# A graph transformer on one core: one low half of FF1 moved from VectorE to GpSimd, an eps step moved, GpSimd's passes cut by graph

## The chip, the core and the metric

The kernel runs on one core of a Trainium2 chip. The metric is device time in microseconds (us). Engines are named as the profile names them: PE is TensorE (matmuls; PEld its weight loads), DVE is VectorE, ACT is ScalarE, POOL is GpSimd, SP is SyncE, which issues the DMAs.

## The reference, cut to what matters

128 independent graphs of 128 nodes with 256 features each. One attention layer ("layer 0") with a residual comes first, then three transformer layers, each of which computes, for every graph:

```python
attn = softmax(where(mask, leaky(x @ aw[:d] [:, None] + x @ aw[d:] [None, :] + b), -inf))
h = layernorm(x + attn @ x, g1[l], beta1[l])                       # eps 1e-5
ff = gelu(h @ W1[l] + b1[l]) @ W2[l] + b2[l]                       # 256 -> 1024 -> 256
x = layernorm(h + ff, g2[l], beta2[l])
```

The output is the result of the third layer plus a residual. All of it is float32; the kernel splits matmul operands into a high and a low half (below).

## The kernel before, in words

**Units and steps.** Four graphs (`T = 4`) form a group, and there are 32 groups. A unit is one group in one of the three layers, so there are 96 units, and one step of the program works on unit `s` in its feed-forward part, while it prepares unit `s + 1` (aggregation, first layernorm), unit `s + 2` (scores and softmax), unit `s + 3` (dot products with the attention vector), and finishes unit `s - 1` (second layernorm). Eight groups are taken through layer 0 of the three, then the same eight through the next, and so on: 24 steps for eight groups (`PER`). Beside this the attention layer 0 of a later group passes through four stages, `early`, `middle`, `late`, `end` (`v0` to `v3`); from step 2 to step 71 a group enters every third step. So steps come in three kinds, which this text calls **A** (`s` = 2, 5, 8, ...: `early` of a new group and `end` of the one before), **B** (`s` = 3, 6, 9, ...: `middle`) and **C** (`s` = 4, 7, 10, ...: `late`). Steps after 73 carry none of it and are called plain.

**Split matmuls.** W1, W2, the normalized input and the gelu are each kept as a float32r high half and a low half (value minus high half), and a product is hi\*hi + hi\*lo + lo\*hi. FF1 (L553, 48 matmuls of 512 columns) makes eight chunks of 128 hidden features x 512 nodes in four PSUM banks; `turn` says which bank a chunk uses, so chunks 4 to 7 reuse the banks of chunks 1, 0, 2 and 3. For each chunk ACT computes the gelu twice from the bank: L674 rounds it into `g_hi`, L676 writes it in full back to the bank. DVE then makes `g_lo` = bank - `g_hi` (L843, `g_low(c)`). PE may overwrite a bank only when its `g_low` is done (L549), and FF2 (L568, 4 x 24 matmuls of 256 columns) waits in its first quarter, chunk by chunk, for `g_lo` of that chunk (L565).

**Order.** Each engine's order is written out by hand in its `body(st)`, and everything between engines is a semaphore. On DVE a step is: sums of the FF2 result (L888), `g_low(0)`, the aggregate's scaling (L904), statistics (L817), `g_low(1)`, mean, variance and eps of the first layernorm (L822, L828), the biases of the softmax (L779 to L791), `g_low(2)`, normalization of `ub` (L927, "z"), `g_low(3)`, in an A step the statistics of the new group's input, `g_low(4)`, `g_low(5)`, in an A step their mean and eps, the statistics of the second layernorm, `g_low(6)`, their mean and eps, `g_low(7)`, and then the rest, which ends with the dot products (L812).

**On POOL** a step is: the power -1/2 for the first layernorm (`rs1`, L1023), which DVE's z waits for; gain and shift of `h` (L1036, L1038) after z; the powers of the other layernorms; masks; and last `affine`, gain and shift of the output `xo` of unit `s - 1` (L356, L358), and in the last layer `residual` (L366). `affine` waits until DVE's dot products of this step are done, so it usually runs into the start of the next step. Each of these passes is one instruction over 128x1024 elements.

Of the kernel before, what the change touches and what calls it, by code (L numbers as in the profile page):

```python
# [13 lines left out]
P = 128  # L14
T = 4
# [21 lines left out]
def build(nc, x, adj, w_fc, w_attn0, attn_w, attn_b, w1, b1, w2, b2, g1, beta1, g2, beta2, out):  # L37
# [44 lines left out]
    with ctx:  # L82
# [37 lines left out]
        et = sb("et", [P, T, P])  # L120
        wfc = et[0:O, :, :].rearrange("p t m -> p (t m)")[:, 0:D]
# [114 lines left out]
        g_lo_ready = sem("g_lo_ready")  # L236
        ff2_done = sem("ff2_done")
# [39 lines left out]
        def live(u):  # L277

            return 0 <= u < U
# [41 lines left out]

        def low_done(eng, st, s, c):

            eng.wait_ge(g_lo_ready, st.nth(s, C, c + 1))
# [22 lines left out]
        def all_graphs(row):  # L347
            return row.unsqueeze(1).to_broadcast((P, T, D))

        def affine(eng, st, u):  # L350


            l = layer(u)
            last = l == L - 1
            eng.wait_ge(z2_ready, st.nth(u))
            eng.tensor_tensor(xo[:, :, :], xo[:, :, :], all_graphs(g2_row[:, l, :]), ALU.mult).then_inc(xo_scaled, 1)  # L356
            eng.wait_ge(xo_scaled, st.nth(u))
            eng.tensor_tensor(xo[:, :, :], xo[:, :, :], all_graphs(beta2_row[:, l, :]),  # L358
                              ALU.add).then_inc(xo_shifted if last else xo_ready, 1)

        def residual(eng, st, u):

            if layer(u) == L - 1:
                eng.wait_ge(xo_shifted, st.nth0(group(u)))
                eng.wait_ge(r_in, 16 * st.nth0(group(u)))
                eng.tensor_tensor(xo[:, :, :], xo[:, :, :], xin[1][:, :, :], ALU.add).then_inc(xo_ready, 1)  # L366
# [121 lines left out]
        def _(pe):  # L488
# [42 lines left out]
            def body(st):  # L531
# [4 lines left out]
                def hidden(c):  # L536
# [11 lines left out]
                    if c >= 4:  # L548
                        low_done(pe, st, s, turn[:4].index(turn[c]))  # L549
# [76 lines left out]
        def _(act):  # L626
# [29 lines left out]
            def body(st):  # L656
# [11 lines left out]
                if live(s):  # L668

                    for c in range(C):  # L670
                        act.wait_ge(ff1_done, st.nth(s, C, c + 1))
                        block_in = bank[turn[c]][:, :]
                        bias = b1_eff[:, layer(s), c:c + 1]
                        act.activation(g_hi[:, c, :], block_in, ACT.Gelu, bias=bias).then_inc(g_hi_ready, 1)  # L674
                        act.wait_ge(g_hi_ready, st.nth(s, C, c + 1))
                        act.activation(block_in, block_in, ACT.Gelu, bias=bias).then_inc(gelu_done, 1)  # L676
                        if c == 1:
                            turned0()
                else:
                    turned0()  # L680
# [4 lines left out]
                if live(s + 2):  # L685
                    act.wait_ge(cc_ready, st.nth(s + 2))
                    exps(e1, ps_s, cc).then_inc(e12_ready, 1)
# [45 lines left out]
        def _(dve):  # L733
# [102 lines left out]
            def body(st):  # L836
# [3 lines left out]
                def g_low(c):  # L840
                    if live(s):
# [69 lines left out]
                g_low(1)  # L911
                if live(s + 1):
                    if not live(s):
                        dve.tensor_copy(spare[:, 2:2 + T], neg_half[:, :])
# [21 lines left out]
                g_low(5)  # L936
                if v0 is not None:
# [4 lines left out]
                second_statistics()  # L942
                g_low(6)
                second_variance()
                g_low(7)
# [58 lines left out]
        def _(pool):  # L1004
# [20 lines left out]
            def body(st):  # L1025
                s = st.s
                v0, v1, v2, v3 = early(s), middle(s), late(s), end(s)
                if live(s + 1):
                    inverse_root(st.nth, s + 1, ve1, rs1, ve1_ready, rs1_ready)
                if live(s + 1):  # L1030
# [5 lines left out]
                    pool.tensor_tensor(h[:, :, :], ub[:, :, :], all_graphs(g1_row[:, l, :]), ALU.mult).then_inc(h_scaled, 1)  # L1036
                    pool.wait_ge(h_scaled, st.nth(s + 1))
                    pool.tensor_tensor(h[:, :, :], h[:, :, :], all_graphs(bb_row[:, l, :]), ALU.add).then_inc(h_ready, 1)  # L1038
# [53 lines left out]
```

## Time and profile before

| | |
|---|---|
| median of 3 runs | 2913.54 us (2911.18 to 2914.14) |
| the profiled execution | 2913.99 us, span 2912.2 us |
| PE busy | 2706.7 us (93%) |
| DVE busy | 2348.0 us (81%) |
| ACT busy | 2148.6 us (74%) |
| POOL busy | 1393.0 us (48%), 806 instructions |
| granted PE clock, mean over the span | 0.969 |

How to read it: the span runs from the first to the last instruction; what the execution's own time has beyond it (1.8 us) lies around it. The first 250 us fill the pipeline. From about 330 us on steps repeat almost to the nanosecond, in periods of three, so one period can be read in detail and multiplied.

### The profile page before, as it was taken

How to read it: one execution, taken by the hardware profiler on the slowest of the kernel's cores; microseconds unless marked ns; L12 is line 12 of the kernel's file. 1: busy time of each engine (PE TensorE's matmuls, PEld its weight loads, DVE VectorE, ACT ScalarE, POOL GpSimd, SP SyncE). 2: the span in 40 equal slices, each digit the busy share in tenths (PEclk: the TensorE clock that was granted, in tenths of full speed). 3: DMA queues.
4: the chain of work that ended last, by engine and by line, in shares of the span. 5: the costliest groups of instructions: out<-in, count | busy, mean ns of one | idle time of the engine just before them, and what ended most of it. 6: DMA issues, size and time to landing. Idle time of an engine off the chain costs nothing.

```text
span 2912.2 us, 52128 instructions
## 1 busy us (share of the span) xinstructions
PE 2706.7 (93%) x16868; PEld 2430.6 (83%) x16868; DVE 2348.0 (81%) x8540; ACT 2148.6 (74%) x3978; POOL 1393.0 (48%) x806
## 2 busy tenths in 40 slices
PE   4268999999999999999999999999999999999998
PEld 3157888888888888888888889888888998999987
DVE  5577798888889888888888888888888887777774
ACT  3357787878778777877777877878787777777775
POOL 2233454444555454444555444545455544444454
PEclk9678999999999999999999999999999999999999
DMA  5322212121322122121223122121222111111211
GB/s 170 111 89 75 78 62 75 63 75 62 97 71 77 62 75 66 63 77 51 90 75 98 61 70 62 58 77 61 89 75 91 57 57 50 50 36 47 64 62 51
DMA packets 120307, 209.64 MB, mean 72 GB/s; under 512 B 12992, under 2 KB 85728, under 8 KB 120032
## 3 DMA queue, kind: packets, MB, share of 16 engines
q1 hardware_dynamic: 120032, 206.26, 22.1%
q8 instruction: 137, 2.24, 0.3%
q14 instruction: 138, 1.13, 0.1%
HBM read 118.15 MB, written 88.08 MB: 71 GB/s over the span
## 4 chain that ended last, share of the span: by engine, by line
PE 74%; DVE 16%; ACT 4%; issue 3%; DMA 1%; POOL 1%; SPq 0%; DVEq 0%; POOLq 0%; ACTq 0%
PE bank L568 35%; PE bank L553 28%; PE ps_u L528 5%; DVE st L817 4%; DVE g_lo L843 4%; PE ps_u L605 2%; PE ps_s L523 2%; DVE ub L904 1%; PE ps_s L515 1%; DVE ve L828 1%; DVE ub L927 1%; DMA xin<-in_x 1%; DVE mv L822 1%; ACT g_hi L674 1%; ACT bank L676 1%
## 5 line engine op out<-in xcount | busy, mean ns | idle before, releaser
L568 PE MATMUL bank<-w_hi,g_hi 128*128 128x256 f32 x3072 | 904.5, 294 | 49.9 <-DVE g_lo L843 49.7
L568 PE MATMUL bank<-w_hi,g_lo 128*128 128x256 f32 x3072 | 875.0, 285 | 0.0
L568 PE MATMUL bank<-w_lo,g_hi 128*128 128x256 f32 x3072 | 874.2, 285 | 0.0
L674 ACT ACTIVATE g_hi<-bank,b_eff 128x512 fp32r<-128x512 f32 x768 | 529.6, 690 | 461.8 <-PE bank L553 456.9
L843 DVE TENSOR_TENSOR g_lo<-bank,g_hi 128x512 fp32r<-128x512 f32 x768 | 518.9, 688 | 211.6 <-ACT bank L676 198.9
L553 PE MATMUL bank<-zt_hi,w_hi 128*128 128x512 f32 x1536 | 646.8, 421 | 12.0 <-DVE vb L888 9.8
L568 PEld LDWEIGHTS bank<-w_hi,g_hi 128*128 128x128 f32 x3072 | 590.0, 192 | 61.8 <-DVE g_lo L843 60.9
L1023 POOL TENSOR_TENSOR rs<-ve,neg_half 128x4 f32<-128x4 f32 x256 | 262.4, 1027 | 726.2 <-DVE ve L828 718.4
L553 PE MATMUL bank<-zt_hi,w_lo 128*128 128x512 f32 x1536 | 608.6, 396 | 0.0
L553 PE MATMUL bank<-zt_lo,w_hi 128*128 128x512 f32 x1536 | 607.7, 396 | 0.0
L568 PEld LDWEIGHTS bank<-w_lo,g_hi 128*128 128x128 f32 x3072 | 590.9, 192 | 0.7
L568 PEld LDWEIGHTS bank<-w_hi,g_lo 128*128 128x128 f32 x3072 | 589.7, 192 | 0.0
L676 ACT ACTIVATE bank<-bank,b_eff 128x512 f32<-128x512 f32 x768 | 508.4, 662 | 25.0
L356 POOL TENSOR_TENSOR xo<-xo,g_row 128x1024 f32<-128x1024 f32 x95 | 226.9, 2388 | 532.4 <-DVE elu_r L985 245.8
L553 PEld LDWEIGHTS bank<-zt_hi,w_hi 128*128 128x128 f32 x1536 | 290.9, 189 | 72.8 <-DVE vb L888 11.7
L553 PEld LDWEIGHTS bank<-zt_hi,w_lo 128*128 128x128 f32 x1536 | 290.3, 189 | 68.2
L553 PEld LDWEIGHTS bank<-zt_lo,w_hi 128*128 128x128 f32 x1536 | 291.4, 190 | 59.2
L1036 POOL TENSOR_TENSOR hb<-ub,g_row 128x1024 f32<-128x1024 f32 x96 | 231.7, 2413 | 222.5 <-DVE ub L927 222.5
L812 DVE CUSTOM_DVE_ANT_0 ub<-xb,aw_row 128x256 f32<-128x256 f32 x768 | 289.4, 432 | 1.3 <-issue 1.0
L646 ACT ACTIVATE e<-ps_s,cc 128x128 f32<-128x128 f32 x512 | 195.5, 382 | 82.3 <-DVE cc L791 81.2
L888 DVE TENSOR_TENSOR vb<-bank,hb 128x512 f32<-128x512 f32 x192 | 129.9, 689 | 142.6 <-PE bank L568 139.0
L1038 POOL TENSOR_TENSOR hb<-hb,bb_row 128x1024 f32<-128x1024 f32 x96 | 229.4, 2389 | 7.5
(95 smaller groups left out, 4265.8 us busy)
## 6 DMA issues: line engine op xcount, KB each, us to landing
xb<-x_scratch SPq DMA_DIRECT2D x96, 512.0 KB, 4.4
x_scratch<-xo SPq DMA_DIRECT2D x69, 512.0 KB, 5.0
xin<-in_x SPq DMA_DIRECT2D x40, 512.0 KB, 4.4
r_scratch<-elu_r SPq DMA_DIRECT2D x32, 512.0 KB, 3.0
xin<-r_scratch SPq DMA_DIRECT2D x32, 512.0 KB, 6.0
out<-xo SPq DMA_DIRECT2D x32, 512.0 KB, 5.3
m<-m_scratch SPq DMA_DIRECT2D x96, 128.0 KB, 2.0
x_scratch<-h SPq DMA_DIRECT2D x24, 512.0 KB, 2.7
```

Of the source, the lines that this page charges most:

```text
L356: eng.tensor_tensor(xo[:, :, :], xo[:, :, :], all_graphs(g2_row[:, l, :]), ALU.mult).then_inc(xo_scaled, 1)
L528: pe.matmul(ps_u[t // 2][:, t % 2 * D:(t % 2 + 1) * D], weights[:, t, :], rows[:, t, :], start=True, stop=True).then_inc(done, 1)
L553: mm = pe.matmul(bank[turn[c]][:, :], w[:, l, k, c * P:(c + 1) * P], z[:, k, :], start=(n == 0), stop=(n == 3 * K1 - 1))
L568: mm = pe.matmul(y, g[:, c, r * P:(r + 1) * P], w[:, l, c, :], start=(c == 0 and n == 0), stop=(c == C - 1 and n == 2))
L646: act.activation(e[:, t, :], src, ACT.Exp, bias=cols[:, 0, t:t + 1])
L674: act.activation(g_hi[:, c, :], block_in, ACT.Gelu, bias=bias).then_inc(g_hi_ready, 1)
L676: act.activation(block_in, block_in, ACT.Gelu, bias=bias).then_inc(gelu_done, 1)
L812: dve.tensor_tensor_reduce(junk[:, j, :], rows[:, t, :], vec(j), 1.0, 0.0, ALU.mult, ALU.add, dot[:, j, t:t + 1]).then_inc(ready, 1)
L843: dve.tensor_tensor(g_lo[:, c, :], bank[turn[c]][:, :], g_hi[:, c, :].bitcast(F32), ALU.subtract).then_inc(g_lo_ready, 1)
L1023: pool.tensor_tensor(rs[:, :], ve[:, :], neg_half[:, :], ALU.pow).then_inc(rs_ready, 1)
L1036: pool.tensor_tensor(h[:, :, :], ub[:, :, :], all_graphs(g1_row[:, l, :]), ALU.mult).then_inc(h_scaled, 1)
L1038: pool.tensor_tensor(h[:, :, :], h[:, :, :], all_graphs(bb_row[:, l, :]), ALU.add).then_inc(h_ready, 1)
```

## The change

It does five things. (1) ACT's second gelu of chunk 1 goes to `g_full`, which is the buffer `e1` (idle at that time) seen as 128x512, not back to the PSUM bank; ACT waits for the last reader of `g_full` before it writes there. (2) `g_low(1)` leaves DVE and becomes POOL's first instruction of a step, 128x512, with a semaphore of its own (`g_lo_pool`). (3) PE's FF1 chunk 4, which reuses chunk 1's bank, waits for ACT's second gelu of chunk 1 and no longer for `g_low(1)`. (4) On DVE, mean and eps of the new group's input (A steps) move from ahead of the second layernorm's statistics to behind `g_low(7)`; the small copy to `spare` that stood there in the fill alone is now issued ahead of the first layernorm's mean in every step. (5) Every 128x1024 pass of POOL (`affine`, `residual`, gain and shift of `h`), and the three of DVE at the very end, are issued as four passes of 128x256.

```diff
+        g_full = e1.rearrange("p t m -> p (t m)")
...
+        POOL_LOW = (1,)
...
         def low_done(eng, st, s, c):
-            eng.wait_ge(g_lo_ready, st.nth(s, C, c + 1))
+            here = sum(k in POOL_LOW for k in range(c + 1))
+            if c + 1 - here:
+                eng.wait_ge(g_lo_ready, st.nth(s, C - len(POOL_LOW), c + 1 - here))
+            if here:
+                eng.wait_ge(g_lo_pool, st.nth(s, len(POOL_LOW), here))
...
-        def all_graphs(row):
-            return row.unsqueeze(1).to_broadcast((P, T, D))
+        def by_graph(eng, dst, src, other, op):
+            for t in range(T):
+                ins = eng.tensor_tensor(dst[:, t, :], src[:, t, :], other(t), op)
+            return ins
...
-            eng.tensor_tensor(xo[:, :, :], xo[:, :, :], all_graphs(g2_row[:, l, :]), ALU.mult).then_inc(xo_scaled, 1)
+            by_graph(eng, xo, xo, lambda t: g2_row[:, l, :], ALU.mult).then_inc(xo_scaled, 1)
             eng.wait_ge(xo_scaled, st.nth(u))
-            eng.tensor_tensor(xo[:, :, :], xo[:, :, :], all_graphs(beta2_row[:, l, :]),
-                              ALU.add).then_inc(xo_shifted if last else xo_ready, 1)
+            by_graph(eng, xo, xo, lambda t: beta2_row[:, l, :], ALU.add).then_inc(xo_shifted if last else xo_ready, 1)
...
                     if c >= 4:
-                        low_done(pe, st, s, turn[:4].index(turn[c]))
+                        owner = turn[:4].index(turn[c])
+                        if owner in POOL_LOW:
+                            pe.wait_ge(gelu_done, st.nth(s, C, owner + 1))
+                        else:
+                            low_done(pe, st, s, owner)
...
-                        act.activation(block_in, block_in, ACT.Gelu, bias=bias).then_inc(gelu_done, 1)
+                        if c in POOL_LOW:
+                            if c > POOL_LOW[0]:
+                                act.wait_ge(g_lo_pool, st.nth(s, len(POOL_LOW), POOL_LOW.index(c)))
+                            elif live(s - 1):
+                                act.wait_ge(g_lo_pool, st.nth(s - 1, len(POOL_LOW)))
+                            act.activation(g_full, block_in, ACT.Gelu, bias=bias).then_inc(gelu_done, 1)
+                        else:
+                            act.activation(block_in, block_in, ACT.Gelu, bias=bias).then_inc(gelu_done, 1)
...
                 if live(s + 2):
                     act.wait_ge(cc_ready, st.nth(s + 2))
+                    if live(s):
+                        act.wait_ge(g_lo_pool, st.nth(s, len(POOL_LOW)))
                     exps(e1, ps_s, cc).then_inc(e12_ready, 1)
...
-                g_low(1)
                 if live(s + 1):
-                    if not live(s):
-                        dve.tensor_copy(spare[:, 2:2 + T], neg_half[:, :])
+                    dve.tensor_copy(spare[:, 2:2 + T], neg_half[:, :])
                     moments(st1, mv1, mv1_ready)
...
                 g_low(5)
+                second_statistics()
+                g_low(6)
+                second_variance()
+                g_low(7)
                 if v0 is not None:
                     if not live(s):
                         dve.tensor_copy(spare[:, 2:2 + T], neg_half[:, :])
                     moments(st4, mv4, mv4_ready)
                     variance(st.nth0, v0, mv4, ve4, mv4_ready, ve4_ready)
-                second_statistics()
-                g_low(6)
-                second_variance()
-                g_low(7)
...
+                def g_low(c):
+                    if live(s):
+                        pool.wait_ge(gelu_done, st.nth(s, C, c + 1))
+                        pool.tensor_tensor(g_lo[:, c, :], g_full, g_hi[:, c, :].bitcast(F32),
+                                           ALU.subtract).then_inc(g_lo_pool, 1)
+
+                g_low(POOL_LOW[0])
                 if live(s + 1):
                     inverse_root(st.nth, s + 1, ve1, rs1, ve1_ready, rs1_ready)
...
-                    pool.tensor_tensor(h[:, :, :], ub[:, :, :], all_graphs(g1_row[:, l, :]), ALU.mult).then_inc(h_scaled, 1)
+                    by_graph(pool, h, ub, lambda t: g1_row[:, l, :], ALU.mult).then_inc(h_scaled, 1)
```

The order of instructions, DVE in an A step, from the first layernorm's statistics on. Before:

```order
936 L817 BN_STATS st<-ub 128x6 x4
937 L843 TENSOR_TENSOR g_lo<-bank,g_hi 128x512
938 L822 BN_AGGR mv<-st 128x2 x4
939 L828 TENSOR_SCALAR ve<-mv 128x4
940 L779 TENSOR_REDUCE small<-ps_s 128x4
```

and with the change:

```order
935 L840 BN_STATS st<-ub 128x6 x4
936 L935 COPY spare<-neg_half 128x4
937 L845 BN_AGGR mv<-st 128x2 x4
938 L851 TENSOR_SCALAR ve<-mv 128x4
939 L802 TENSOR_REDUCE small<-ps_s 128x4
```

The `g_lo` subtraction has gone and a copy of 128x4 to `spare` stands in its place. Further on in the same step, from the statistics of the new group's input (`xin`) to `g_low(7)`. Before:

```order
949 L817 BN_STATS st<-xin 128x6 x4
950 L843 TENSOR_TENSOR g_lo<-bank,g_hi 128x512 x2
951 L822 BN_AGGR mv<-st 128x2 x4
952 L828 TENSOR_SCALAR ve<-mv 128x4
953 L817 BN_STATS st<-vb 128x6 x4
954 L843 TENSOR_TENSOR g_lo<-bank,g_hi 128x512
955 L822 BN_AGGR mv<-st 128x2 x4
956 L828 TENSOR_SCALAR ve<-mv 128x4
957 L843 TENSOR_TENSOR g_lo<-bank,g_hi 128x512
```

and with the change:

```order
948 L840 BN_STATS st<-xin 128x6 x4
949 L866 TENSOR_TENSOR g_lo<-bank,g_hi 128x512 x2
950 L840 BN_STATS st<-vb 128x6 x4
951 L866 TENSOR_TENSOR g_lo<-bank,g_hi 128x512
952 L845 BN_AGGR mv<-st 128x2 x4
953 L851 TENSOR_SCALAR ve<-mv 128x4
954 L866 TENSOR_TENSOR g_lo<-bank,g_hi 128x512
955 L845 BN_AGGR mv<-st 128x2 x4
956 L851 TENSOR_SCALAR ve<-mv 128x4
```

The first of the two pairs of mean (`mv`) and eps (`ve`) has moved from ahead of the statistics of `vb` to behind the last subtraction; the next instruction after it is `zt_lo` in both.

POOL, from the end of an A step (`affine`) into the B step after it, with the semaphores that each waits for. Before:

```order
103 L356 TENSOR_TENSOR xo<-xo,g_row 128x1024 [waits z2_ready,dots0_ready,dots_ready]
104 L358 TENSOR_TENSOR xo<-xo,beta_row 128x1024 [waits xo_scaled]
105 L1023 TENSOR_TENSOR rs<-ve,neg_half 128x4 [waits ve1_ready]
106 L1036 TENSOR_TENSOR hb<-ub,g_row 128x1024 [waits v_done,z_ready]
107 L1038 TENSOR_TENSOR hb<-hb,bb_row 128x1024 [waits h_scaled]
```

and with the change:

```order
131 L358 TENSOR_TENSOR xo<-xo,g_row 128x256 [waits z2_ready,dots0_ready,dots_ready]
132 L358 TENSOR_TENSOR xo<-xo,g_row 128x256 x3
133 L358 TENSOR_TENSOR xo<-xo,beta_row 128x256 [waits xo_scaled]
134 L358 TENSOR_TENSOR xo<-xo,beta_row 128x256 x3
135 L1053 TENSOR_TENSOR g_lo<-e,g_hi 128x512 [waits gelu_done]
136 L1044 TENSOR_TENSOR rs<-ve,neg_half 128x4 [waits ve1_ready]
137 L358 TENSOR_TENSOR hb<-ub,g_row 128x256 [waits v_done,z_ready]
138 L358 TENSOR_TENSOR hb<-ub,g_row 128x256 x3
139 L358 TENSOR_TENSOR hb<-hb,bb_row 128x256 [waits h_scaled]
140 L358 TENSOR_TENSOR hb<-hb,bb_row 128x256 x3
```

Between `affine` and the power for the first layernorm (`rs`, waiting for `ve1_ready`) there is now the subtraction of chunk 1, and each pass is four instructions, of which the first carries the wait.

## Rows read from the trace of the kernel before

**Rows 1.** Busy time of PE, from the page.

```profile
PE 2706.7 (93%) x16868; PEld 2430.6 (83%) x16868; DVE 2348.0 (81%) x8540; ACT 2148.6 (74%) x3978; POOL 1393.0 (48%) x806
```

**Rows 2.** Waits of PE from 300 us on: us in total, times, longest.

```profile
PE bank L568 <- DVE g_lo L843: 48.7, 45, 1.9
```

**Rows 3.** Timeline of ACT: start, us, engine, line, operation [idle before <-releaser].

```profile
1042.45 0.69 ACT L674 ACTIVATE g_hi<-bank,b_eff 128x512 fp32r<-128x512 f32 x1 [2.26 <-PE bank L553]
...
1046.30 0.66 ACT L676 ACTIVATE bank<-bank,b_eff 128x512 f32<-128x512 f32 x1
...
1072.61 0.69 ACT L674 ACTIVATE g_hi<-bank,b_eff 128x512 fp32r<-128x512 f32 x1 [1.85 <-PE bank L553]
...
2641.67 0.69 ACT L674 ACTIVATE g_hi<-bank,b_eff 128x512 fp32r<-128x512 f32 x1 [2.33 <-PE bank L553]
...
2667.97 0.69 ACT L674 ACTIVATE g_hi<-bank,b_eff 128x512 fp32r<-128x512 f32 x1 [2.35 <-PE bank L553]
```

**Rows 4.** Timeline of PE in a step A, around its wait.

```profile
1057.17 0.28 PE L568 MATMUL bank<-w_lo,g_hi 128*128 128x256 f32 x1
1057.29 0.28 PE L568 MATMUL bank<-w_hi,g_lo 128*128 128x256 f32 x1
1059.31 0.39 PE L568 MATMUL bank<-w_hi,g_hi 128*128 128x256 f32 x1 [1.74 <-DVE g_lo L843]
```

**Rows 5.** Windows on PE: us, busy us (x instructions), granted clock, DMA share, GB/s.

```profile
1056.20:1059.60 3.40, 1.66 (x14) 1.00 0.00 0
1059.65:1063.05 3.40, 3.07 (x15) 0.50 0.00 0
1230.30:1233.70 3.40, 2.94 (x23) 1.00 0.00 0
```

**Rows 6.** Timeline of DVE in the same step A, and a copy in the B after it.

```profile
1047.60 0.69 DVE L843 TENSOR_TENSOR g_lo<-bank,g_hi 128x512 fp32r<-128x512 f32 x1
...
1048.61 0.17 DVE L828 TENSOR_SCALAR ve<-mv 128x4 f32<-128x4 f32 x1
...
1050.69 1.37 DVE L927 TENSOR_SCALAR ub<-ub,mv,rs 128x256 f32<-128x256 f32 x4
...
1055.22 0.37 DVE L822 BATCH_NORM_AGGREGATE mv<-st 128x2 f32<-128x6 f32 x4
1055.62 1.50 DVE L828 TENSOR_SCALAR ve<-mv 128x4 f32<-128x4 f32 x1
1057.04 1.39 DVE L817 BATCH_NORM_STATS2 st<-vb 128x6 f32<-128x256 f32 x4
...
1059.65 0.69 DVE L843 TENSOR_TENSOR g_lo<-bank,g_hi 128x512 fp32r<-128x512 f32 x1
...
1090.32 0.51 DVE L781 COPY small<-dots 128x4 f32<-128x4 f32 x1
```

**Rows 7.** Timeline of POOL through steps A and B.

```profile
1039.45 2.40 POOL L356 TENSOR_TENSOR xo<-xo,g_row 128x1024 f32<-128x1024 f32 x1 [9.64 <-DVE elu_r L985]
...
1054.71 2.39 POOL L1038 TENSOR_TENSOR hb<-hb,bb_row 128x1024 f32<-128x1024 f32 x1
...
1065.66 1.01 POOL L1023 TENSOR_TENSOR rs<-ve,neg_half 128x4 f32<-128x4 f32 x1 [3.83 <-DVE ve L828]
1066.63 0.19 POOL L1018 TENSOR_TENSOR spare<-neg_half 128x1 f32<-128x1 f32 x1
...
1071.68 2.37 POOL L356 TENSOR_TENSOR xo<-xo,g_row 128x1024 f32<-128x1024 f32 x1 [2.62 <-DVE dots L812]
...
1088.88 1.93 POOL L1048 TENSOR_SCALAR m_new<-m_new 128x512 bf16<-128x512 bf16 x1
```

**Rows 8.** Timelines of POOL and DVE in a step B of the last layer.

```profile
905.79 2.39 POOL L366 TENSOR_TENSOR xo<-xo,xin 128x1024 f32<-128x1024 f32 x1
...
906.85 1.36 DVE L828 TENSOR_SCALAR ve<-mv 128x4 f32<-128x4 f32 x1
```

**Rows 9.** Timeline of PE: first matmul of chunk 7 in a step B.

```profile
1083.81 0.40 PE L553 MATMUL bank<-zt_hi,w_hi 128*128 128x512 f32 x1
```

More of the change, by code:

```diff
@@ L236, in build @@
         g_lo_ready = sem("g_lo_ready")
+        g_lo_pool = sem("g_lo_pool")
         ff2_done = sem("ff2_done")
@@ L365, in residual @@
                 eng.wait_ge(r_in, 16 * st.nth0(group(u)))
-                eng.tensor_tensor(xo[:, :, :], xo[:, :, :], xin[1][:, :, :], ALU.add).then_inc(xo_ready, 1)
+                by_graph(eng, xo, xo, lambda t: xin[1][:, t, :], ALU.add).then_inc(xo_ready, 1)
         block = ctx.enter_context(nc.Block())
@@ L840, in g_low @@
                 def g_low(c):
-                    if live(s):
+                    if live(s) and c not in POOL_LOW:
                         dve.wait_ge(gelu_done, st.nth(s, C, c + 1))
@@ L1035, in body @@
                     h = hb[(s + 1) % 2]
-                    pool.tensor_tensor(h[:, :, :], ub[:, :, :], all_graphs(g1_row[:, l, :]), ALU.mult).then_inc(h_scaled, 1)
+                    by_graph(pool, h, ub, lambda t: g1_row[:, l, :], ALU.mult).then_inc(h_scaled, 1)
                     pool.wait_ge(h_scaled, st.nth(s + 1))
-                    pool.tensor_tensor(h[:, :, :], h[:, :, :], all_graphs(bb_row[:, l, :]), ALU.add).then_inc(h_ready, 1)
+                    by_graph(pool, h, h, lambda t: bb_row[:, l, :], ALU.add).then_inc(h_ready, 1)
                 if live(s - 1):
```

## The prediction

> **What bounds the kernel now.** I read the page first, then PE's waits, then one period of three steps engine by engine, because the steps repeat. PE is busy for 93% of the span [rows 1], and the rest is mostly the fill; so a gain must come from PE's remaining waits, or from its clock. From 300 us on PE waits for one thing: `g_lo`, in FF2, 45 times, 48.7 us in all [rows 2]. The timeline puts these waits in the A steps, two in each of 23, and nowhere else. I count time in a step from ACT's first gelu, "t0": 1042.45 in this A, 1072.61 in the B after it, so this A lasts 30.16 us, while a plain step lasts 26.30 [rows 3]. An A has no PE work that a plain step lacks; the 3.86 us between them are what can be won there.
>
> They have two parts. FF2's matmuls follow each other by 0.12 us; chunk 6 is due at 1057.41, three after it chunk 7 at 1057.77 (t0 + 15.3), but they start at 1059.31 and, once `g_low(7)` ends at 1060.34, at 1060.39 [rows 4, 6]. That is 2.6 us late. Then the granted clock falls to 0.50, which is 1.2 GHz of 2.4, for 3.4 us [rows 5]: 15 matmuls go through in it, which take 0.12 us each at full clock, so 1.3 to 1.6 us are lost. Before it fell PE had stood idle for 1.74 us [rows 4]. In 6 of the 23 A steps, like the one at 1230, it did not fall [rows 5]. The mean loss of an A is 2.6 + 1.3 x 17/23 = 3.6 us, 83 us in 23 steps.
>
> Why is DVE late in an A? It has a sixth piece of work there, and one small instruction costs far more than its work: the eps (L828), 128x4, takes 0.17 us in one place and 1.50 in the other [rows 6]. The long one ends at 1057.12, 0.02 after POOL's 128x1024 pass, which ran from 1054.71 to 1057.10 [rows 7]. The same shows at 906.85: 1.36 us, to 908.21, with POOL's pass ending at 908.18 [rows 8]. So an eps that meets a pass of POOL waits for its end. Subtractions with one input in PSUM run beside such passes undisturbed [rows 6, 7].
>
> **The change, part by part, in an A step.**
>
> *The mean and eps of the new group leave the path.* From 1055.22 to 1057.04 [rows 6]: 1.82 us ahead of both late subtractions.
>
> *`g_low(1)` leaves DVE.* It took 0.61 us, from 1047.60 to where the mean starts [rows 6]. But the copy to `spare` takes its place, and a copy waits for POOL too: the one at 1090.32 took 0.51 us and ended at 1090.83 [rows 6], POOL's mask pass at 1090.81 [rows 7]. POOL's subtraction starts when ACT's full gelu of chunk 1 is done, 1046.30 + 0.66 [rows 3], plus 0.1 to wake, at 1047.1, and DVE comes to the copy at 1047.60, so it meets it. No row shows a 128x512 pass of POOL with two inputs. 128x1 takes 0.19 and 128x1024 2.39 [rows 7], so a straight line gives 0.19 + 1.10 = **1.29 us**; bounds are half of 2.39, 1.20, and 1.37, the line plus a gap of 0.08. It ends at 1048.4, the mean starts at 1048.35 and not at 1048.21. The removal gains nothing, it loses 0.14.
>
> *The second layernorm's eps.* It now meets POOL's passes for `h`, since these are longer in sum. One pass of 128x256: the line gives 0.19 + 0.55 = 0.74; where POOL's next instruction waits for nothing it can start 0.04 before the end of the one before (1066.67 against 1066.63 [rows 7]). I take **0.70 us**, bounds 0.60 (a quarter of 2.39, all overhead hidden) and 0.82 (0.74 and a gap of 0.08, none hidden). Eight passes for `h` then take 5.7 us, not 4.9, and end at 1058.05; the eps comes at 57.9 and waits for 0.15.
>
> *Together:* `g_low(7)` ends at 1060.34 - 1.82 + 0.14 + 0.15 = 1058.8, chunk 7 starts 1.1 us late, and an A lasts 27.4 us. PE then idles some 1.1 us. No row shows the clock after so short a wait; since even 1.7 leaves it up in 6 of 23, I take it to stay (if it fell in all 17, that would be 22 us less). That saves 3.6 - 1.1 = 2.5 us in 17 of the A steps: **42 us**. In the 6 others `affine` and `residual` of the last layer come before: 12 passes from t0 - 3.0 (1039.45 [rows 7]) are 8.4 and two gaps, to t0 + 5.6, and with POOL's subtraction the first eps is free at 7.0, not 6.3. Chunk 7 is 1.7 late and the clock may fall in half of them: 1.3 saved, **8 us**.
>
> *PE's earlier leave for chunk 4* is worth nothing: PE doesn't wait there now [rows 2]. ACT's gelu into SBUF is priced at 0.03 us a step, as `g_hi` takes 0.69 and the bank 0.66 [rows 3]; ACT waits for PE before most chunks. If that slack went it would be 3 us in all. FF2's first quarter, which reads POOL's part, has its chunk 6 at 1057.41 [rows 4], 9 us behind that subtraction.
>
> **What it costs, in B steps.** POOL's queue now stands in the way of z: `affine`, subtraction, power, and only then DVE's z, `g_low(3)`, and PE's chunk 7, which reuses that bank and is due at 1083.81, t0 + 11.2 [rows 9]. `affine` starts when DVE's last dot product of A is done, 1071.68 now [rows 7], some 1.2 us earlier with the change (1.5 won, less the moved pair); but t0 of B is then 1069.85, so it is at t0 + 0.6, where it was at -0.9. Eight short passes, 5.7 us, subtraction and power (1.0 [rows 7]) with their gaps lead to t0 + 8.9; z and `g_low(3)` take 1.37 and 0.61 more [rows 6]: 10.9, just in time. In the last layer `residual` adds 2.8: 12 passes end at 9.2, the subtraction at 10.6, the power at 11.7 and `g_low(3)` at 13.7. PE waits 2.5 us, and its clock falls in most of them, 1.0 more. There are 9 such B steps (unit s - 2 in the last layer): **-31 us**. In C steps `affine` waits for no dot products of a new group and starts earlier; I count nothing there.
>
> *The end.* Three passes of POOL for the last but one unit have no other work beside them; as 12 they take 8.4 instead of 7.2 us: **-1 us**.
>
> **Sum:** 42 + 8 - 31 - 1 = 18 us less than the profiled execution's 2914.0 (which is 0.5 above the median): **2896 us**.
>
> Everything hangs on the length of a short pass. At 0.60, with the subtraction at 1.20, A saves 2.65 everywhere (61), B loses 1.2 x 9 = 11: 2865. At 0.82 and 1.37, A saves 41 and in the last layer loses 3, B of the last layer waits 4.0 and 1.3 for the clock (-48), other B steps 0.6 (-8), the end 2: 2934. Zero lies near 0.76.
>
> On this price the Trainium skill speaks against the change. GPSIMD Engine Reference, section 3.1, gives 4497 ns for a float32 tensor_tensor of 2048 elements. With this trace's 2.39 us for 1024 that would be 2.06 ns an element and a fixed 0.28 us, so 0.81 for a short pass, an estimate, by which the sum would be about 2931. No row here shows a pass of 2048 or of 256 elements, so the trace neither bears this out nor denies it.
>
> **The rivals.**
>
> 1. *Long passes: slower.* POOL becomes the bound in the last layer's B steps, as above. For it: in the B at 900 the passes end late already and eps and z with them [rows 8]. Against it: the overlap of 0.04 [rows 7]. It decides from 0.76 us a pass: up to 2934. Chance 0.26. (The page just named stands for this one.)
> 2. *Short passes.* If overhead hides behind the pass before, B hardly waits: 2865. For it: the same overlap. Chance 0.22.
> 3. *Cutting doesn't open the port.* In every row where the eps waits, POOL's next instruction was itself waiting. With four passes queued the next one may begin before DVE gets in; the eps then waits for all four. The passes for `h` end 0.8 us later than now, and the second eps with them, in some 65 steps other than A; half of it hidden by slack, that is 26 us, so 2922. Chance 0.12.
> 4. *The forecast,* 2885 to 2907. Chance 0.40.
>
> **How the numbers follow.** A difference under 0.2%, 6 us, can't be told from none. Faster are case 4 and 2: 0.62. Cases 1 and 3 lie mostly above 2919: slower 0.30, same 0.08. The range goes from the short end, 2862, to the long end, 2935.
>
> **What would show it.** PE's wait for `g_lo` in FF2 falls from 2.1 to about 1.1 us an A, without a fall of the clock behind it; A lasts about 27.4. POOL's 128x256 passes follow each other by 0.70, its subtraction takes 1.29, and the copy to `spare` lasts about 0.8 in A. A new wait of PE appears at FF1's chunk 7 (L553's line) in 9 B steps, about 2.5 us. Wrong would be: no such wait, or A steps still near 30 us, or an eps that outlasts one short pass.

## The result, and the profile after

The changed kernel takes **2872.77 us** (median of 4 runs, 2872.0 to 2874.63), the one before 2913.56 beside it: ratio 0.9862, interval 0.9845 to 0.988. It is faster by 41 us; forecast were 18, with a range from 2862 to 2935 that holds it. The profiled execution took 2872.99 us, span 2871.2, granted clock 0.975 in place of 0.969.

The page, busy time (after; before in [rows 1]):

```profile
PE 2687.5 (94%) x16868; PEld 2406.8 (84%) x16868; DVE 2327.7 (81%) x8548; ACT 2148.2 (75%) x3978; POOL 1698.0 (59%) x2141
```

PE's waits from 300 us on, as in [rows 2]: us in total, times, longest.

```profile
PE bank L582 <- DVE g_lo L866: 11.6, 23, 0.5
PE bank L567 <- DVE g_lo L866: 10.7, 10, 1.3
...
PE bank L567 <- POOL g_lo L1053: 3.2, 8, 0.4
```

The 48.7 us of waiting in FF2 have become 11.6, one wait of at most 0.5 us in each A. New are waits in FF1 (L567), for DVE's and for POOL's part.

An A step in detail, the one with the same number as in [rows 3 to 7]. ACT's first gelu of this step and of the next:

```profile
1028.65 0.69 ACT L688 ACTIVATE g_hi<-bank,b_eff 128x512 fp32r<-128x512 f32 x1 [2.27 <-PE bank L567]
...
1055.98 0.69 ACT L688 ACTIVATE g_hi<-bank,b_eff 128x512 fp32r<-128x512 f32 x1 [0.63 <-PE bank L567]
```

It lasts 27.33 us, where it took 30.16 [rows 3]. DVE in it, as in [rows 6]:

```profile
1033.80 0.77 DVE L935 COPY spare<-neg_half 128x4 f32<-128x4 f32 x1
1034.48 0.37 DVE L845 BATCH_NORM_AGGREGATE mv<-st 128x2 f32<-128x6 f32 x4
...
1036.97 1.37 DVE L948 TENSOR_SCALAR ub<-ub,mv,rs 128x256 f32<-128x256 f32 x4
...
1041.50 1.40 DVE L840 BATCH_NORM_STATS2 st<-vb 128x6 f32<-128x256 f32 x4
...
1044.03 0.21 DVE L851 TENSOR_SCALAR ve<-mv 128x4 f32<-128x4 f32 x1
1044.15 0.68 DVE L866 TENSOR_TENSOR g_lo<-bank,g_hi 128x512 fp32r<-128x512 f32 x1
```

and POOL, as in [rows 7], with the start of `affine` in the B step:

```profile
1033.26 1.29 POOL L1053 TENSOR_TENSOR g_lo<-e,g_hi 128x512 fp32r<-128x512 f32 x1 [1.94 <-ACT e L695]
...
1041.40 2.81 POOL L358 TENSOR_TENSOR hb<-hb,bb_row 128x256 f32<-128x256 f32 x4
...
1056.27 2.81 POOL L358 TENSOR_TENSOR xo<-xo,g_row 128x256 f32<-128x256 f32 x4 [2.62 <-DVE dots L835]
1059.15 2.82 POOL L358 TENSOR_TENSOR xo<-xo,beta_row 128x256 f32<-128x256 f32 x4
```

The copy takes 0.77 us, since it meets POOL's subtraction (1.29), and lets the mean start at t0 + 5.83. The statistics of `vb` come right behind `g_low(5)`, the second eps takes 0.21, and `g_low(7)` ends at 1044.83, t0 + 16.18, where it ended at t0 + 17.89. The timeline of PE shows its wait, the window behind it the clock (us, busy us, granted clock, DMA share, GB/s):

```profile
1044.89 0.39 PE L582 MATMUL bank<-w_hi,g_hi 128*128 128x256 f32 x1 [0.49 <-DVE g_lo L866]
```

```profile
1044.90:1048.30 3.40, 3.40 (x28) 1.00 0.00 0
```

The clock is 1.00 there, 2.4 GHz, as in all 23 A steps but the one that ends eight groups (a wait of 1.88 us at the turn to the next eight, after which it fell once).

POOL's groups by form, all of the span: busy us, mean ns of one | idle before.

```profile
L358 POOL TENSOR_TENSOR hb<-hb,bb_row 128x256 f32<-128x256 f32 x384 | 274.5, 747 | 7.5
...
L358 POOL TENSOR_TENSOR xo<-xo,g_row 128x256 f32<-128x256 f32 x380 | 267.6, 736 | 470.3 <-DVE elu_r L1006 224.6 <-DVE dots L835 137.2 <-ACT xo L667 88.9
...
L1053 POOL TENSOR_TENSOR g_lo<-e,g_hi 128x512 fp32r<-128x512 f32 x96 | 123.7, 1288 | 178.5 <-ACT e L695 178.5
```

One step B of the last layer, t0 = 888.38. POOL:

```profile
888.73 2.81 POOL L358 TENSOR_TENSOR xo<-xo,g_row 128x256 f32<-128x256 f32 x4 [2.78 <-issue]
891.62 2.84 POOL L358 TENSOR_TENSOR xo<-xo,beta_row 128x256 f32<-128x256 f32 x4
894.54 2.82 POOL L358 TENSOR_TENSOR xo<-xo,xin 128x256 f32<-128x256 f32 x4
897.30 1.31 POOL L1053 TENSOR_TENSOR g_lo<-e,g_hi 128x512 fp32r<-128x512 f32 x1
898.56 1.04 POOL L1044 TENSOR_TENSOR rs<-ve,neg_half 128x4 f32<-128x4 f32 x1
```

DVE in it:

```profile
893.53 0.25 DVE L935 COPY spare<-neg_half 128x4 f32<-128x4 f32 x1
...
894.10 0.39 DVE L851 TENSOR_SCALAR ve<-mv 128x4 f32<-128x4 f32 x1
...
895.33 0.65 DVE L808 TENSOR_TENSOR small<-small 128x4 f32<-128x4 f32 x1
896.01 0.66 DVE L810 SCALAR_TENSOR_TENSOR small<-small 128x4 f32<-128x4 f32 x1
896.71 0.66 DVE L813 TENSOR_TENSOR cc<-small 128x4 f32<-128x4 f32 x1
897.29 0.15 DVE L814 SCALAR_TENSOR_TENSOR cc<-small 128x4 f32<-128x4 f32 x1
...
899.64 1.38 DVE L948 TENSOR_SCALAR ub<-ub,mv,rs 128x256 f32<-128x256 f32 x4 [1.59 <-POOL rs L1044]
```

PE in it, with the window behind its second wait:

```profile
898.75 0.47 PE L567 MATMUL bank<-zt_hi,w_hi 128*128 128x512 f32 x1 [0.43 <-POOL g_lo L1053]
...
901.67 0.51 PE L567 MATMUL bank<-zt_hi,w_hi 128*128 128x512 f32 x1 [1.28 <-DVE g_lo L866]
```

```profile
901.70:905.10 3.40, 3.40 (x23) 1.00 0.03 8
```

`affine` starts at t0 + 0.35 and its eight passes take 5.73 us, `residual`'s four begin at 6.16, the subtraction at 8.92, the power ends at 11.22, z starts at 11.26. PE waits 0.43 for POOL's subtraction ahead of chunk 6 (that chunk reuses chunk 2's bank, which POOL doesn't read, but `low_done(2)` waits for the low half of chunk 1 as well), and after six matmuls 1.28 for `g_low(3)` ahead of chunk 7. The clock stays at 1.00. DVE's three operations at 895.33 to 896.71, 128x4, take 0.65 each here and 0.16 elsewhere. They cost nothing in this step: DVE is through with them and with `g_low(2)` at 898.04, and then waits 1.59 for the power.

The sums over the steps of each kind (from ACT's first gelu to that of the next step), both profiled executions, worked out from their timelines of ACT; the columns add up to the spans, 2912.2 and 2871.2:

| steps | n | before, us | after, us | won | forecast |
|---|---|---|---|---|---|
| A | 17 | 508.4 | 464.1 | 44.3 | 42 |
| A, last layer's `residual` in it | 6 | 183.4 | 168.1 | 15.3 | 8 |
| B | 14 | 376.5 | 376.8 | -0.3 | 0 |
| B, last layer's `residual` in it | 9 | 243.1 | 261.1 | -18.0 | -31 |
| C | 23 | 654.0 | 654.0 | 0 | 0 |
| plain | 21 | 551.5 | 549.9 | 1.6 | 0 |
| end (last step) | 1 | 34.6 | 36.4 | -1.8 | -1 |
| start and fill | 5, and what is ahead of them | 360.8 | 360.8 | 0 | 0 |

### The profile page after: what moved, and what is told of

Same layout as the page of the kernel before. It is cut to its first block, busy times and chain, and to the rows that moved or that the text cites. A ratio compares the mean times of both kernels' runs of the same rounds, so it can differ in the third digit from the quotient of the medians.

```text
span 2871.2 us, 54613 instructions
## 1 busy us (share of the span) xinstructions
PE 2687.5 (94%) x16868; PEld 2406.8 (84%) x16868; DVE 2327.7 (81%) x8548; ACT 2148.2 (75%) x3978; POOL 1698.0 (59%) x2141
## 4 chain that ended last, share of the span: by engine, by line
PE 69%; DVE 13%; POOL 6%; ACT 5%; issue 4%; DMA 2%; SPq 0%; DVEq 0%; POOLq 0%; ACTq 0%
PE bank L582 32%; PE bank L567 26%; PE ps_u L538 5%; DVE st L840 3%; DVE g_lo L866 3%; POOL xo L358 3%; PE ps_u L619 2%; POOL rs L1044 2%; PE ps_s L533 2%; DVE ub L927 1%; DVE ub L948 1%; PE ps_s L525 1%; POOL hb L358 1%; DMA xin<-in_x 1%; ACT g_hi L688 1%
## 5 line engine op out<-in xcount | busy, mean ns | idle before, releaser
L582 PE MATMUL bank<-w_hi,g_hi 128*128 128x256 f32 x3072 | 891.6, 290 | 12.2 <-DVE g_lo L866 11.6
L567 PE MATMUL bank<-zt_hi,w_hi 128*128 128x512 f32 x1536 | 649.3, 423 | 26.0 <-DVE g_lo L866 10.7
L567 PE MATMUL bank<-zt_hi,w_lo 128*128 128x512 f32 x1536 | 609.4, 397 | 0.0
L567 PE MATMUL bank<-zt_lo,w_hi 128*128 128x512 f32 x1536 | 607.8, 396 | 0.0
L582 PEld LDWEIGHTS bank<-w_hi,g_hi 128*128 128x128 f32 x3072 | 579.3, 189 | 22.1 <-DVE g_lo L866 20.7
L866 DVE TENSOR_TENSOR g_lo<-bank,g_hi 128x512 fp32r<-128x512 f32 x672 | 449.8, 684 | 174.4 <-ACT bank L697 165.1
L582 PEld LDWEIGHTS bank<-w_lo,g_hi 128*128 128x128 f32 x3072 | 579.7, 189 | 0.7
L582 PEld LDWEIGHTS bank<-w_hi,g_lo 128*128 128x128 f32 x3072 | 579.0, 188 | 0.0
L358 POOL TENSOR_TENSOR xo<-xo,g_row 128x256 f32<-128x256 f32 x380 | 267.6, 736 | 470.3 <-DVE elu_r L1006 224.6
L697 ACT ACTIVATE bank<-bank,b_eff 128x512 f32<-128x512 f32 x672 | 444.9, 662 | 21.8
L358 POOL TENSOR_TENSOR hb<-ub,g_row 128x256 f32<-128x256 f32 x384 | 271.9, 740 | 205.7 <-DVE ub L948 205.7
L567 PEld LDWEIGHTS bank<-zt_hi,w_hi 128*128 128x128 f32 x1536 | 291.5, 190 | 94.7 <-DVE g_lo L866 23.4
L567 PEld LDWEIGHTS bank<-zt_hi,w_lo 128*128 128x128 f32 x1536 | 290.6, 189 | 68.3
L567 PEld LDWEIGHTS bank<-zt_lo,w_hi 128*128 128x128 f32 x1536 | 291.7, 190 | 57.3
L358 POOL TENSOR_TENSOR hb<-hb,bb_row 128x256 f32<-128x256 f32 x384 | 274.5, 747 | 7.5
L358 POOL TENSOR_TENSOR xo<-xo,beta_row 128x256 f32<-128x256 f32 x380 | 266.5, 733 | 7.4
```

What stands on the lines that cost most here:

```text
L358: ins = eng.tensor_tensor(dst[:, t, :], src[:, t, :], other(t), op)
L567: mm = pe.matmul(bank[turn[c]][:, :], w[:, l, k, c * P:(c + 1) * P], z[:, k, :], start=(n == 0), stop=(n == 3 * K1 - 1))
L582: mm = pe.matmul(y, g[:, c, r * P:(r + 1) * P], w[:, l, c, :], start=(c == 0 and n == 0), stop=(c == C - 1 and n == 2))
L866: dve.tensor_tensor(g_lo[:, c, :], bank[turn[c]][:, :], g_hi[:, c, :].bitcast(F32), ALU.subtract).then_inc(g_lo_ready, 1)
```

## The experiments

Two questions: which part of the change brings the 41 us, and what makes the last layer's B steps cost 2.0 us each instead of 3.4. The kernel before ran beside each at 2913.8 to 2914.8 us.

### Parts alone and in pairs

**1. The eps move alone.** The low half is back on DVE and the passes are whole:

```diff
-        POOL_LOW = (1,)
+        POOL_LOW = ()
...
-            for t in range(T):
-                ins = eng.tensor_tensor(dst[:, t, :], src[:, t, :], other(t), op)
-            return ins
+            return eng.tensor_tensor(dst[:, :, :], src[:, :, :], other(0).unsqueeze(1).to_broadcast((P, T, D)), op)
```

> The kernel before with one edit: mean and eps of the new group behind g_low(7). Theory (the eps pair is the whole gain; the low half on POOL and the short passes cost more than they bring): g_low(7) in A ends 1.82 us earlier, A lasts about 27.1, no fall of the clock; B of the last layer 27.6, since affine starts later against t0. 67 us less, 6 back: about 2852. Rival (the low half on POOL or the short passes are needed for the gain): at or above the changed kernel, 2873 or more.

Measured: 2854.72 us, ratio 0.9796 (0.978 to 0.9812), 18 us below the whole change. An A takes 27.26 us, a B of the last layer 27.73. PE's waits:

```profile
PE bank L580 <- DVE g_lo L862: 11.2, 25, 0.5
...
PE bank L565 <- DVE g_lo L862: 1.8, 8, 0.2
```

So the rest of the change costs 18 us; by steps, 11.5 of them are in the last layer's nine B steps (261.1 us in the table above, 249.6 here).

**2. Eps move and short passes**, the low half on DVE:

```diff
-        POOL_LOW = (1,)
+        POOL_LOW = ()
```

> The changed kernel with g_low(1) back on DVE: eps moved and short passes alone. Theory: without POOL's 1.3 us ahead of the power, the last layer's B steps last about 27.9 instead of 29.1; A about 27.1; plain steps as before. About 2857. Rival (DVE needs the 0.61 us of g_low(1)): A steps 0.6 longer than in the changed kernel, 2873 + 14 - 11, about 2876.

Measured: 2859.74, ratio 0.9816 (0.98 to 0.9833), 5 us above run 1. Where the eps has moved, short passes add nothing. A B of the last layer takes 27.80, against 29.02 in the whole change: most of what the low half on POOL costs is there.

**3. Eps move and low half on POOL**, whole passes:

```diff
-            for t in range(T):
-                ins = eng.tensor_tensor(dst[:, t, :], src[:, t, :], other(t), op)
-            return ins
+            return eng.tensor_tensor(dst[:, :, :], src[:, :, :], other(0).unsqueeze(1).to_broadcast((P, T, D)), op)
```

> The changed kernel with POOL's passes of 128x1024 again: eps moved and the low half of chunk 1 on POOL. Theory: A about 27.2, affine and residual end 1.4 us earlier in the last layer's B steps, which last about 27.9; about 2857. Rival (short passes open the way for DVE's small instructions, so wide ones hold the copy, the eps and the softmax biases for up to 2.4 us each): B of the last layer 29 or more and some loss in C, 2873 or more.

Measured: 2863.42, ratio 0.9827 (0.9811 to 0.9844). The low half on POOL costs 9 us here.

**4. Short passes alone.** The eps is back ahead of `second_statistics()`, and the low half on DVE:

```diff
-        POOL_LOW = (1,)
+        POOL_LOW = ()
...
-                second_statistics()
-                g_low(6)
-                second_variance()
-                g_low(7)
                 if v0 is not None:
...
                     variance(st.nth0, v0, mv4, ve4, mv4_ready, ve4_ready)
+                second_statistics()
+                g_low(6)
+                second_variance()
+                g_low(7)
```

> The kernel before with one edit: POOL's passes by graph. Theory: in A the first eps of the new group waits for at most one short pass, about 0.2 us instead of 1.33, g_low(7) is 1.4 late instead of 2.6, the clock stays up, A lasts about 27.7; B of the last layer about 27.9. About 2867. Rival (an eps waits for all four queued passes): A as before, about 2925.

Measured: 2867.4, ratio 0.9842 (0.9826 to 0.9859). An A takes 27.72: the eps in its old place gets in between two short passes, and takes 0.26 us there in the A at 1025 us.

**5. The low half on POOL alone** (the eps back as in run 4, the passes whole as in run 1):

```diff
-            for t in range(T):
-                ins = eng.tensor_tensor(dst[:, t, :], src[:, t, :], other(t), op)
-            return ins
+            return eng.tensor_tensor(dst[:, :, :], src[:, :, :], other(0).unsqueeze(1).to_broadcast((P, T, D)), op)
...
-                second_statistics()
...
                     variance(st.nth0, v0, mv4, ve4, mv4_ready, ve4_ready)
+                second_statistics()
```

> The kernel before with one part: the low half of chunk 1 on POOL (with the copy to spare in every step), eps in its old place, wide passes. Theory: DVE gives up 0.61 us and waits 0.77 in the copy; the new group's eps still waits for POOL's wide pass; A as before (about 30), other steps as before: 2911 to 2918. Rival (DVE's relief is what helps): A 0.6 shorter, 2900.

Measured: 2919.38, ratio 1.0015 (1.0006 to 1.0025): 4.6 us slower than before. 0.6 us less work on DVE buys nothing.

**6. Low half and short passes**, the eps in its old place:

```diff
-                second_statistics()
...
                     variance(st.nth0, v0, mv4, ve4, mv4_ready, ve4_ready)
+                second_statistics()
```

> The changed kernel with the eps pair back in its old place. Theory: in A the pair costs its 0.49 us of work and a wait of 0.1 to 0.7 for a short pass, so A lasts about 28.0 instead of 27.3; B of the last layer 28.4 instead of 29.0. 2882 if the clock stays up, up to 2900 if it falls after the longer wait.

Measured: 2881.98, ratio 0.9886 (0.987 to 0.9903).

Together, us less than the kernel before ran beside them: eps 59, short passes 46, both 54; each of these with the low half on POOL as well: 50, 33, 41; the low half alone -5. The eps move and the short passes are two cures for one wait, so they don't add up, and the low half costs 5 to 14 us beside whatever else is there.

### What POOL's passes do to DVE's small operations

Both runs of this part take up the three operations of 0.65 us in the B step above, which have two operands in SBUF.

**7. The power first**, ahead of POOL's subtraction, in the whole change:

```diff
-                g_low(POOL_LOW[0])
                 if live(s + 1):
                     inverse_root(st.nth, s + 1, ve1, rs1, ve1_ready, rs1_ready)
+                g_low(POOL_LOW[0])
```

> The changed kernel with POOL's power for the first layernorm ahead of its subtraction of chunk 1. Theory A (DVE's small instructions with two inputs in SBUF, 0.16 us each, wait for POOL's pass as the eps does: L808 to L813 took 0.65 each in a B step of the last layer): the copy is free, but the softmax biases now meet the subtraction, wait about 1.0, and every step has g_low(3) 0.5 too late for chunk 7: 2900 or more. Theory B (only one-input work waits): A 0.6 shorter, B of the last layer 1.1 shorter, about 2850.

Measured: 2887.42 (one of its four runs took 6851.8, for which nothing here gives a reason; without it the median is 2886.99), ratio 0.9903 (0.9883 to 0.9923): 14 to 15 us slower than the change, in the direction of theory A, at half its size. POOL and then DVE in a plain step:

```profile
2430.98 1.02 POOL L1044 TENSOR_TENSOR rs<-ve,neg_half 128x4 f32<-128x4 f32 x1 [5.73 <-DVE ve L851]
2431.98 1.30 POOL L1053 TENSOR_TENSOR g_lo<-e,g_hi 128x512 fp32r<-128x512 f32 x1
```

```profile
2431.87 0.16 DVE L810 SCALAR_TENSOR_TENSOR small<-small 128x4 f32<-128x4 f32 x1
2432.07 1.23 DVE L813 TENSOR_TENSOR cc<-small 128x4 f32<-128x4 f32 x1
```

The subtraction now runs from 2431.98 to 2433.28, and the `cc` operation, which takes 0.16 elsewhere, ends at 2433.30. z comes 0.47 us later than under the change (t0 + 8.79 for 8.32), and each of the 21 plain steps is 0.36 longer, each A step 0.47. In the last layer's B steps the earlier power wins 0.33.

**8. The residual later.** The eps move alone, and `residual` taken from behind `affine` to between the power and z of the next step:

```diff
                     inverse_root(st.nth, s + 1, ve1, rs1, ve1_ready, rs1_ready)
+                if live(s - 2) and s - 2 < U - 1:
+                    residual(pool, st, s - 2)
...
                     affine(pool, st, s - 1)
-                    residual(pool, st, s - 1)
```

> The kernel before with the eps pair moved, and POOL's residual of the last layer put behind the next step's power, not ahead of it. Theory: what is left in B of the last layer (27.7 against 26.9) is the eps that waits for residual's wide pass and the power behind it; it goes, 9 x 0.8 = 7 us: about 2848. Rival (the output's DMA, issued 1 to 4 us later, holds ACT's next write of xo or the next load): same as without it, 2855, or more.

Measured: 2901.57, ratio 0.9956 (0.9939 to 0.9972), 47 us above run 1: a miss. POOL and DVE in a C step of the last layer, t0 = 743.24:

```profile
749.65 1.03 POOL L1042 TENSOR_TENSOR rs<-ve,neg_half 128x4 f32<-128x4 f32 x1 [4.81 <-DVE ve L847]
750.65 2.40 POOL L374 TENSOR_TENSOR xo<-xo,xin 128x1024 f32<-128x1024 f32 x1
```

```profile
750.34 0.16 DVE L804 TENSOR_TENSOR small<-small 128x4 f32<-128x4 f32 x1
750.54 0.16 DVE L806 SCALAR_TENSOR_TENSOR small<-small 128x4 f32<-128x4 f32 x1
750.73 2.33 DVE L809 TENSOR_TENSOR cc<-small 128x4 f32<-128x4 f32 x1
752.99 0.15 DVE L810 SCALAR_TENSOR_TENSOR cc<-small 128x4 f32<-128x4 f32 x1
```

During the power (1.03 us) two such operations took 0.16 each; the third meets the residual and takes **2.33 us**, to 0.01 past its end. So z starts at t0 + 10.4 and not at 8.3, in the last layer's A, B and C steps alike, where in run 1 only B was late (t0 + 9.6). The place that looked idle on POOL was the one where DVE has its small operations on the path to z.

### Where the margins are

**9. The second statistics late.** The eps move alone, and in A steps the statistics and eps of the second layernorm behind `g_low(7)`:

```diff
-                if v0 is not None:
+                if v0 is None:
...
+                else:
+                    g_low(6)
+                    g_low(7)
+                    if live(s - 1):
+                        dve.wait_ge(v_done, st.nth(s - 1, 2))
+                        statistics(vb, st2, st2_ready)
...
                     variance(st.nth0, v0, mv4, ve4, mv4_ready, ve4_ready)
+                    second_variance()
```

> The eps move alone, and in A steps also the statistics and the eps of the second layernorm behind g_low(7). Theory: after the eps move the 1.39 us of these statistics are what still makes PE wait in an A, so g_low(7) ends near t0 + 14.2 instead of 15.98, PE waits for nothing there and an A lasts 26.4 instead of 27.3: 17 x 0.9 and 6 x 1.2 saved. DVE's dot products then end some 0.8 us later in the step after, so affine starts later and the B steps of the last layer lose up to 0.7 each, 6 in all. 2854.7 - 22 + 6 = 2839 us. Rival: DVE has no idle time left in A and B together, what A wins B loses in full: 2854.

Measured: 2882.92, ratio 0.9892 (0.9877 to 0.9907), 28 us above run 1. Neither theory: `g_low(7)` does end at t0 + 14.25 and FF2 waits for nothing, but a new wait stands at t0 + 21.5. In this kernel's waits and in the timeline of its A step at 1115 us:

```profile
PE ps_s L531 <- DVE e L817: 41.8, 24, 2.0
```

```profile
1138.66 0.66 PE L531 MATMUL ps_s<-ident,e 128*128 128x128 f32 x4 [1.80 <-DVE e L817]
```

PE waits there for the softmax weights `e`. The chain of waits leads back from them over the dots, `nm` and POOL's powers to the eps that was moved: an A has a second path, with hardly any slack, which the first had hidden. The windows behind two of these waits, of 1.80 us and of 1.92:

```profile
1138.70:1142.10 3.40, 3.40 (x29) 1.00 0.01 2
1389.60:1393.00 3.40, 3.40 (x22) 0.69 0.00 0
```

The clock stays at 1.00 after the first and falls after the second; it fell in 3 of the 22 such steps besides the one at the turn.

**10. The residual behind `h`.** The eps move alone; `residual` as four passes, and in B steps behind the passes for `h`:

```diff
+                if live(s - 2) and v1 is not None:
+                    residual(pool, st, s - 2)
                 if live(s - 1):
                     inverse_root(st.nth, s - 1, ve2, rs2, ve2_ready, rs2_ready)
...
                     affine(pool, st, s - 1)
-                    residual(pool, st, s - 1)
+                    if v0 is None:
+                        residual(pool, st, s - 1)
```

> The eps move alone, with the residual of a unit whose step was an A taken out of POOL's queue ahead of the power and issued, as four passes of 128x256, behind the passes for h in the B step after. Theory (a pass of POOL with two inputs costs what DVE's copies and operations with two SBUF inputs meet of it, and nothing else): the B steps of the last layer go from 27.73 to 26.9 us, since nothing of POOL now meets the eps and the softmax's small operations, and the second eps gets in between short passes; 9 x 0.8 = 7 us: 2847. The moved residual of the run before missed because it was put between the power and z, in C and A steps too, where those small operations stand. Rival: in its new place it holds the second eps and with it g_low(7), zt_lo and the masks: no gain, 2855 to 2862.

Measured: 2856.34, ratio 0.9804 (0.979 to 0.9817), no gain over run 1. z is on time (t0 + 8.25), but the last layer's B steps take 27.87 us: the residual now stands ahead of the second layernorm's power, and PE waits 0.4 to 1.1 us in each of them for the softmax weights `e`. The chain of waits in one of them (start, us, what):

```profile
896.23 0.68 POOL xo L375
...
897.38 1.44 POOL xo L375 x2
898.82 0.99 POOL rs L1044
```

**11. Runs 9 and 10 together.**

```diff
+                    g_low(7)
...
+                        statistics(vb, st2, st2_ready)
...
+                if live(s - 2) and v1 is not None:
+                    residual(pool, st, s - 2)
```

> Both of the last two. Theory: the losses of the later affine in the last layer's B steps are gone too, so the two add up to more than their sum: A 26.4, B 26.9 in every layer: 2854.7 - 22 - 7 = 2826 us. Rival (DVE is the bound over A and B together): no better than the better of the two.

Measured: 2883.34, ratio 0.9897 (0.9882 to 0.9912). A 28.44 us, last layer's B 27.83: as the two misses would have it.

**12. The whole change with the residual behind `h`** in B steps (the edit of run 10):

```diff
+                if live(s - 2) and v1 is not None:
+                    residual(pool, st, s - 2)
                 if live(s - 1):
                     inverse_root(st.nth, s - 1, ve2, rs2, ve2_ready, rs2_ready)
```

> The whole change, with the residual of B steps moved behind the passes for h. Theory: the 18.0 us that the last layer's B steps lose under the change come from the residual's four passes ahead of the subtraction and the power, 2.8 us of queue and the 1.5 us that they add to DVE's small operations; moved, z comes at t0 + 8.5 as in the other B steps and a B lasts 27.0 instead of 29.0: 2872.8 - 18 = 2855 us. Rival (it is the subtraction and the short affine passes that make B late): 2868 or more.

Measured: 2871.04, ratio 0.985 (0.9835 to 0.9865). PE's waits:

```profile
PE ps_s L533 <- DVE e L821: 15.5, 10, 1.8
...
PE bank L567 <- DVE g_lo L866: 0.7, 4, 0.2
```

FF1's waits in the last layer's B steps are all but gone (10.7 and 3.2 us before this edit, 0.7 now) and z starts at t0 + 8.53, where it started at 11.26: so it was the residual's place in POOL's queue that made z late. But waits for `e` stand in their place, one of 1.5 to 1.8 us in each of these nine steps, since the power for the second layernorm is late instead. They last 28.78 us each, where they took 29.02. The number is the rival's, the cause is the theory's.

## Why the prediction was right or wrong

**The place of the loss, and the A steps: right.** 42 us were forecast for 17 A steps, 44.3 came. Each piece is in the trace: copy to `spare` 0.77 (0.8 forecast), mean at t0 + 5.83 (5.9), second eps 0.21 in place of 0.17 (a wait of 0.15 forecast), chunk 7 about 0.9 late (1.1), no fall of the clock. Run 1 shows that the eps move alone does all of it (A 27.26), and run 4 that the short passes alone would have done most (27.72).

**"The removal gains nothing": right.** Run 5 is 4.6 us slower, not faster.

**The prices of POOL: right.** Short passes start every 0.70 us (0.74 busy, 0.04 of it over the next), the subtraction takes 1.29. From the 4497 ns of the Trainium skill's GPSIMD Engine Reference, section 3.1, and the 2.39 us of this trace came an estimate of 0.81 for a short pass; the measured 0.74 busy decides.

**The last layer's B steps: the step that failed. -31 us were forecast, -18.0 measured, and most of the difference is the fall of the clock put into this term.** The queue was as forecast, and everything in it came 0.3 to 0.5 us early: `affine` at t0 + 0.35 (0.6 forecast), z at 11.26 (11.7), `g_low(3)` done at 13.24 (13.7). That is 0.4 of the 1.4 us a step. The other 1.0 was "its clock falls in most of them", and it fell in none (the turn to the next eight groups aside). The forecast took the fall from a wait of 1.74 us in an A, and had B's 2.5 us as one wait; it came as 0.43 and 1.28, with six matmuls between. Why the clock fell after the one and not after the other no run shows.

**The A steps with a residual: 8 us forecast, 15.3 measured.** Here too the forecast had the clock fall in half of them, 0.65 a step on average, 3.9 us; it did so only at the turn. Some 1.8 us more are that their chunk 7 is only 0.3 us later than in other A steps, not 0.6; the last 1.6 are not traced to a piece. The two clock terms together, 9 and 3.9 us, are 12.9 of the 23 us by which the forecast missed.

**The end and the rest:** -1.8 for the -1 forecast; plain steps give 1.6 that weren't in the sum.

**The rivals.** Long passes (0.26): refuted by 0.70. Short passes (0.22): its time, 2865, is nearer than the forecast's, 8 us off against 23, but by luck: its reason is wrong, since passes are 0.70 and B does wait. That cutting doesn't open the port (0.12): refuted at 893.53 and 894.10, where copy and eps take 0.25 and 0.39 us while POOL has passes queued, and by run 4, where the cutting alone wins 46 us. "Everything hangs on the length of a short pass" was wrong: that length was hit to 0.01 us, and the time missed by 23 us, over the clock and some tenths of lateness. So the range holds the result by luck too: its ends were worked out from other lengths of a pass, which did not occur.

**Not seen ahead:** that the change carries a part that costs. The forecast put the copy's 0.14 us on the low half's account and stopped; its 1.3 us in POOL's queue were booked under B, where they are part of the 18. The eps move alone, at 2854.7 us, beats both kernels.

## What to carry to other kernels

Before an operation is moved to an engine that looks idle, list what is queued behind it there and which engine waits for that; a thing moved later on one path needs the next path's slack checked too (runs 8, 9, 10 and 12 each removed the wait they aimed at and met the next one). When a change bundles several cures, time each alone: two here cure the same wait, and a third costs. Don't put a fall of the clock into a sum on the evidence of one kind of wait.

## What the runs showed of the hardware

**A VectorE operation with two SBUF operands waits for the end of a float32 GpSimd pass with two inputs, however small it is.** 128x4 operations of 0.16 us took 0.65 beside 128x256 passes, 1.23 beside a 128x512 subtraction and 2.33 beside a 128x1024 pass, each ending within 0.02 us of the pass where only one stood there (runs 7 and 8). The prediction had counted copies and the eps alone. A power of 128x4 on GpSimd, 1.03 us long, held none of them. Neither did POOL's mask pass, a TENSOR_SCALAR of bf16 with one tensor as input, as long as they came in its first 1.3 us. With the change, POOL and then DVE:

```profile
823.34 1.93 POOL L1077 TENSOR_SCALAR m_new<-m_new 128x512 bf16<-128x512 bf16 x1
```

```profile
824.01 0.16 DVE L808 TENSOR_TENSOR small<-small 128x4 f32<-128x4 f32 x1
824.40 0.16 DVE L813 TENSOR_TENSOR cc<-small 128x4 f32<-128x4 f32 x1
```

In all 30 mask passes of that trace that such operations met, they took 0.16; but a copy that came 1.45 us into the mask pass at 1577.20 took 0.50 and ended with it. The Trainium skill's page SBUF — State Buffer, section "SBUF: two separate sides", says that such an operation and a GpSimd one that reads SBUF exclude each other for a whole instruction; the float32 passes agree with that, the power and the mask pass do not show it.

**Queued GpSimd passes let VectorE in between.** With four 128x256 passes in the queue and nothing to wait for, a copy took 0.25 us and an eps 0.39, not the 2.8 of all four.

**The length of a wait doesn't settle whether PE's clock falls.** Before, a wait of 1.6 to 1.9 us, in most A steps with one of 0.2 to 0.5 behind it, was followed by 1.2 GHz in 17 of 23 A steps [rows 4, 5]; in run 9 a wait of 1.7 to 2.1 us at another place of the step was followed by it in 3 of 22, and in run 12 nine waits of 1.5 to 1.8 us by none. What else decides it stays open.
